# Transformer block on one core: q ahead of k in the first batch, row loads from one queue, dummy transposes around the projections, and new places for jobs of the first and last batches

## The reference, cut to what matters

```python
xn = _layernorm(x, axis=-1)
q, k, v = (split_heads(einsum('bsh,oh->bso', xn, w) * s + b) for w, s, b in ...)
scores = jnp.einsum('bhqd,bhkd->bhqk', q, k) / jnp.sqrt(jnp.float32(HEAD))
ctx = jnp.einsum('bhqk,bhkd->bhqd', jax.nn.softmax(scores, axis=-1), v)
attn = einsum('bsh,oh->bso', ctx, w_o) * s_o + b_o
h = jnp.concatenate([xn, -xn], axis=-1)
h = jax.nn.relu(s0 * (h @ w0)) * 2
h = jax.nn.relu(s1 * (h @ w1)) * 2
x = x + attn + s2 * (h @ w2)
```

## Time and profile before

| | us |
|---|---|
| median of three timed runs (296.8 to 298.94) | 297.9 |
| profiled execution, its own time | 294.85 |
| span of the profiled execution | 293.0 |
| PE busy | 273.5 (93%) |
| DVE busy | 246.0 (84%) |
| ACT busy | 219.3 (75%) |
| POOL busy | 151.0 (52%) |

### The profile page before, as it was taken

How to read it: one execution, slowest core, us unless ns; L and a number is a source line. 1 busy time by engine, 2 the same in 40 slices (tenths; PEclk the granted TensorE clock), 3 DMA queues, 4 the chain that set the end, 5 groups by cost and what they waited for, 6 DMA issues and landing times.

```text
span 293.0 us, 10539 instructions
## 1 busy us (share of the span) xinstructions
PE 273.5 (93%) x3924; PEld 185.3 (63%) x3924; DVE 246.0 (84%) x495; ACT 219.3 (75%) x456; POOL 151.0 (52%) x376
## 2 busy tenths in 40 slices
PE   4659699999999999999999999999999999999893
PEld 4235375757676776767585867677676758675442
DVE  4654969998989899998989898999999898999522
ACT  2431349889888888979888888888897988777880
POOL 6045446464929293746657382927475575421311
PEclk9557989999999999999999999999999999999999
DMA  5032403232323324142413232332424132320001
GB/s 134 28 122 60 144 19 113 62 111 68 100 76 86 112 58 131 51 126 67 127 36 112 80 106 91 97 101 57 130 60 120 42 106 74 107 74 4 22 22 36
DMA packets 27395, 23.95 MB, mean 82 GB/s; under 512 B 4674, under 2 KB 24146, under 8 KB 27346
## 3 DMA queue, kind: packets, MB, share of 16 engines
q1 hardware_dynamic: 27218, 22.89, 26.2%
q10 hardware_dynamic: 128, 0.39, 0.4%
...
## 4 chain that ended last, share of the span: by engine, by line
PE 88%; DVE 6%; ACT 2%; issue 1%; ACTq 1%; DMA 1%; POOL 0%; POOLq 0%
PE work L984 21%; PE work L1057 20%; PE max_bank L965 14%; PE exp_bank L970 9%; PE work L1089 5%; PE work L1030 4%; PE work L1014 3%; PE work L1098 3%; PE work L1021 3%; DVE neg_max L725 2%; PE work L1010 2%; PE work L999 2%; PE work L992 2%; DVE r_lo L752 1%; PE work L1009 1%
## 5 line engine op out<-in xcount | busy, mean ns | idle before, releaser
L725 DVE TENSOR_REDUCE neg_max<-max_bank 128x2 f32<-128x512 f32 x256 | 167.9, 678 | 22.0 <-PE max_bank L965 18.7
L566 ACT ACTIVATE probs<-exp_bank 128x512 f32<-128x512 f32 x256 | 145.4, 597 | 27.2 <-PE exp_bank L970 22.6
L965 PE MATMUL max_bank<-k_rows,q_rows 48*128 48x256 f16 x512 | 88.7, 271 | 1.5 <-DVE neg_max L725 1.3
L970 PE MATMUL exp_bank<-q_rows,k_rows 51*128 51x256 bf16 x512 | 87.6, 271 | 1.3 <-ACT probs L566 1.2
L984 PE MATMUL work<-probs,v_ext 128*32 128x256 f32 x1024 | 65.0, 383 | 0.2
L1057 PE MATMUL work<-r_hi,w 64*128 64x256 f16 x512 | 61.5, 274 | 0.1
L1057 PE MATMUL work<-r_lo,w 64*128 64x256 f16 x512 | 61.2, 273 | 0.0
L965 PEld LDWEIGHTS max_bank<-k_rows,q_rows 48*128 48x128 bf16 x512 | 40.2, 95 | 25.4 <-DVE neg_max L725 13.8
L970 PEld LDWEIGHTS exp_bank<-q_rows,k_rows 51*128 51x128 f16 x512 | 39.5, 94 | 9.5 <-ACT probs L566 3.3
L752 DVE SCALAR_TENSOR_TENSOR r_lo<-work,r_hi 128x512 f16<-128x512 f32 x64 | 43.3, 679 | 1.7 <-ACT r_hi L619 1.7
L619 ACT ACTIVATE r_hi<-work 128x512 f16<-128x512 f32 x64 | 36.9, 603 | 9.5 <-PE work L1057 3.9
...
## 6 DMA issues: line engine op xcount, KB each, us to landing
...
q_scratch<-q_part SPq DMA_DIRECT2D x16, 192.0 KB, 2.0
...
q_rows<-max_rows SPq DMA_DIRECT2D x64, 6.0 KB
...
```

What stands on the lines that cost most here:

```text
L566: nc.scalar.activation(probs[h // HALF][:, h % HALF, :, :].rearrange("p k q -> p (k q)"), exp_bank[h % 2][:, :], ACT.Exp, scale=EXP_SCALE) ...
L725: nc.vector.tensor_reduce(out=neg_max[:, h // HALF, h % HALF // 2, h % 2, :], in_=max_bank[h % 2][:, :].rearrange("p (q k) -> p q k", q=TT ...
L965: last = mm(max_bank[h % 2][:, t * SEQ:(t + 1) * SEQ], q[:, t * P:(t + 1) * P], k, start=True, stop=True)
L970: last = mm(exp_bank[h % 2][:, t * SEQ:(t + 1) * SEQ], k[:, t * P:(t + 1) * P], q, start=True, stop=True)
```

## The change

In batch 0, ACT scales and cuts q ahead of k; SP stores q ahead of k and also issues the four k loads, behind the q loads; DVE computes the rest of q ahead of the weights of layer 0, and both low parts ahead of the statistics of batch 1. On PE, four transposes of the identity stand between turn_x and the projections of batch 0, 22 more behind the bias matmul, and all of them write max_bank[1]. In the tables, all four quarters of layer 1 of batch 0 stand ahead of the first maxima score, with turn_x of batch 1 between the third and the second, and the projections of batch 1 behind the fourth. The low part r1_lo of the first half stands ahead of the first neg_max. maxT1 goes to bank 2 (with q and the contexts) instead of bank 0. In the batches between, some jobs change places on POOL, SP and DVE (xT_lo later on POOL; rows and max1 earlier on SP; o behind layer 2 on PE). In the last batch, maxT1 comes a head earlier, v_ext is copied later, and y on POOL stands behind the last ctxn.

```diff
@@ tables @@
-PE_LATER = {("l1_0", 0): -3, ("l1_0", 15): -1, ("l0_1", 0): -2, ("o", 14): 3, ("l0_0", 0): -2, ("xT", 0): -1, ("xT", 1): -5,
...
+            ("xT", 1): -5, ("l2", 15): -2, ("maxT1", 15): -1, ("l1_0", 0): -14, ("l1_0", 1): -1, ("l1_0", 15): -1,
...
-BANK = {"l0a": 0, "l0b": 3, "l1a": 3, "l1b": 1, "q": 2, "k": 0, "ctx0": 2, "ctx1": 2, "maxT0": 1, "maxT1": 0, "xT": 0, "v": 0,
+BANK = {"l0a": 0, "l0b": 3, "l1a": 3, "l1b": 1, "q": 2, "k": 0, "ctx0": 2, "ctx1": 2, "maxT0": 1, "maxT1": 2, "xT": 0, "v": 0,
@@ SP @@
             load_x(1)
+            store_q(sp, 0)
             store_k(sp, 0)
-            store_q(sp, 0)
             load_q(sp, 0)
+            load_k(sp, 0)
@@ ACT @@
-            scale_k(0)
-            cut_k_hi(0)
             scale_q(0)
             cut_q_hi(0)
+            scale_k(0)
             cut_q_mid(0)
+            cut_k_hi(0)
             second_layer_weights(1)
-            load_k(act, 0)
@@ DVE @@
             split_xT(nc.vector, dve, 0)
+            rest_q(nc.vector, dve, 0)
+            first_layer_weights()
+            split_q(nc.vector, dve, 0)
             split_k(nc.vector, dve, 0)
-            first_layer_weights()
-            rest_q(nc.vector, dve, 0)
             token_stats(1)
-            split_q(nc.vector, dve, 0)
             mean_and_variance(1)
@@ PE @@
-                    nc.tensor.transpose(exp_bank[0][:, 0:P], ident[:, :], ident[:, :])
+                    nc.tensor.transpose(max_bank[1][:, 0:P], ident[:, :], ident[:, :])
...
             turn_x(0)
+            keep_warm(4)
             project_qk(0, 0)
             project_qk(0, 1)
             pe.wait_ge(bv_cols_ready, 1)
             mm(exp_bank[1][:, 0:HID], bv_cols[:, :], w_sb[:, 3, :], start=True, stop=True).then_inc(bias_psum, 1)
+            keep_warm(22)
```

62 lines of the change are left out of this document (30 added, 32 removed), and 6 rows, old and new, of the table PE_LATER.

## The result

The changed kernel is slower: the median of four runs is 301.02 us (299.42 to 302.54), that of the kernel before in the same session 297.35; the ratio is 1.016, with a 95% interval of 1.0116 to 1.0204. In this document a median takes all runs of a kernel, and a ratio leaves out those more than 1.5% above the fastest run of their kernel. The profiled execution took 300.83 us, its span is 299.0. So the change costs 3.7 by the medians and 4.8 by the ratio, where the prediction had a gain of 2.0.

What follows compares the result with a forecast made beforehand. PE's own work bounds the middle, so the head was the lever: the first exp score moves from 42.20 to 40.2, a gain of 2.0, with 0 behind it, so 297.9 becomes 295.9 us; range 293.7 to 299.2.

Steps and rivals of the forecast that it cites:

- Step 8: Slots 0 to 17, first neg_max to first exp score: 15.1 us instead of 16.23, with a clock fall as today.
- Step 7: Row loads on one queue: rows land at 23.4, wait up to 0.6 covered by DVE; first neg_max at 25.1.
- T17: Start of the first exp score, slot 17; forecast at 40.2 us, against 42.20 in the kernel before.
- Behind T17: After the first exp score: 0 taken, by DVE's spare time of 14 in 190; possible loss 1.5 us together.
- Steps 1 to 3: Head: four transposes free, projections and bias at full clock to 10.23, 22 transposes 4.68 us to 14.91.
- Steps 5 and 6: Head: layer 1 starts at about 17.5, runs whole until about 21.6; batch 1's projections end at 22.85.
- The tail: Batch 15: y behind the last ctxn ends at 289.60, before the last outs at 290.17; costs 0, bound 0.7.
- B: Head rival: clock falls at 8.5, returns midway through the 22 transposes; T17 43.4, time 299.1 us, chance 0.20.
- C: Head rival: clock falls and the 22 transposes don't bring it back; T17 47.5, time 303.2 us, chance 0.08.
- D: Rival: head's gain lost to later batches (1.5), rows (0.5) or max rows; time 297.9 us, chance 0.09.

Runs made afterwards that it cites:

- e2: The kernel before with the 4 and 22 dummy transposes alone, nothing else of the change: 294.74 us, ratio 0.9953.
- e6: The changed kernel's straight code and dummies, with all ten tables and the bank of maxT1 from the kernel before: 294.96 us.
- e8: e2 with 11 dummy transposes added in the last 17 slots: 295.13 us.
- e7: e2 with the third and fourth quarters of layer 1 ahead of the first maxima score and r1_lo ahead of the first neg_max: 297.10 us, ratio 1.0008.
- e13: e6 with batch 0's layer 1, then batch 1's projections, ahead of the first maxima score, batch 1's turn_x moved, r1_lo ahead of the first neg_max: 297.41 us.
- e4: The changed kernel with 11 dummy transposes in the last 17 slots, its head unedited: 300.22 us.
- e11: The changed kernel with the old slots of batches 14 and 15 on PE, ACT and DVE: 301.44 us.
- e3: The changed kernel with 28 more dummy transposes between the maxima scores of batch 0: 302.57 us.
- e12: e6 with the changed tables of POOL and SP: 296.91 us.
- e14: The changed kernel with layer 1's last quarters, batch 1's projections and turn, its layer 0 and v among batch 0's slots, r1_lo later: 299.50 us.
- e17: e14 with the old tables of POOL and SP too: 296.99 us, ratio interval 0.9956 to 1.0043.

## Why the prediction was wrong

The direction failed, and with it the range: 301.0 lies above 299.2, and no case of the prediction had this mechanism. The step that failed is the eighth, slots 0 to 17 (15.1 predicted, 16.90 measured), with the seventh ahead of it, the first neg_max (25.1 predicted, 26.54 measured), and the term behind T17 (0 predicted, 1.75 measured). The profiled executions side by side:

| kernel | first maxima score | first neg_max | from there to T17 | half clock in it, about |
|---|---|---|---|---|
| before | 25.55 | 25.97 | 16.23 | 3.5 |
| prediction | 23.4 | 25.1 | 15.1 | 3.5 |
| changed | 24.73 | 26.54 | 16.90 | 13.5 |
| e2 | 23.53 | 23.96 | 15.64 | 3.5 |
| e6 | 23.75 | 24.17 | 16.09 | 3.5 |
| e8 | 24.66 | 25.08 | 17.40 | 7 |
| e7 | 26.96 | 28.40 | 16.05 | 10 |
| e13 | 26.68 | 29.07 | 15.82 | 10 |

- Steps 1 to 3, the dummies. Right in what they do: layer 0 starts at 15.20 (14.91 predicted), straight behind them, and ran at full clock. That the start is hit so well is luck, for two errors cancel: the projections and the bias matmul ran at the pace of half clock, and the 22 transposes started at 11.80 and not at 10.23; and they took 3.46, not 4.68. Alone the dummies gain 1.4 to 1.8 (e2), against 2.0 that the prediction gave to the whole.
- Steps 5 and 6, to the end of the projections of batch 1: 22.85 predicted, 24.36 measured. Layer 1 started at 18.53 and not at 17.5: it accumulates into the bank from which the second r_lo is read, so it waits for both r_lo. And a quarter that follows a quarter takes 1.11 from start to start, not the 0.89 that the earlier trace rows show between scores.
- Step 7, rows and first neg_max. The q store was issued at 14.32, not 12.7, because the projections were still at half clock; the k rows landed near 24.7 and not 23.4. No run shows the 1.7 that the prediction took from the issue of a load to its landing: the last k load was issued by 22.19, and PE's wait for the k rows ended at 24.73, 2.5 later. The first neg_max came at 26.54, not 25.1. What was missed is not only the size but what it does: the prediction let DVE be late and called the rows' wait covered. PE, with layer 1 done, had nothing left to do during that lateness except two scores. Against e6, which leaves this work among the scores, T17 of the changed kernel is 3.18 later, and 2.37 of that are there at the first neg_max.
- Step 8. Taking two quarters of layer 1 out of the slots was booked as a saving of PE time in a stretch that DVE sets. It took away the work with which PE had filled its waits. With it gone PE idles for over 2 us at the first neg_max, and some 13.5 us at half clock follow. The prediction expected a fall near the length of today's and bounded T17 by 41.4; measured are 43.4 to 46.8 in the changed kernel and in those with its head unedited (e4, e11). e7 and e13 show that these places, without the rest of the new tables, make the first neg_max and T17 late, with the long wait and some 10 us at half clock. What half clock costs in the slots shows in e8, which has the head of e2: 17.40 with some 7 us of it, 15.64 with 3.5. In e7 and e13 the slots take no longer than before (16.05, 15.82): that fits half clock taking back what the moved quarters had saved there, and T17 is late by about as much as the first neg_max. That the wait is what brings the fall is not shown; in e3 the clock fell with the wait cut to 0.66.
- Behind T17. Zero was taken, with 1.5 as the bound; the profiles show 1.75, and e12 has 1.46 over e6 for POOL and SP alone. The spare time of DVE was the wrong row to lean on. PE's idle time between T17 and the last maxima score grows from 0.43 to 1.52, of which 1.02 are waits for q rows, which come through POOL and SP, and the first maxima score of a batch has nothing beside it to hide that; the other 0.66 is PE's own work taking longer in its new order.
- The tail. y behind the last ctxn cost nothing, as predicted: the last output still waited for the projection (0.80 of idle, 0.81 before). The 3.0 of the profile after are no part of the change.
- The rivals. The first half of B came true: the projections ran at half clock, and the transposes started at 11.80, where B has 11.85. But the clock was back for the transposes, and layer 0 started at 15.20, not at 18.2; that B's T17, 43.4, is the measured one is luck. B and C also price a transpose at half clock at 0.425, twice the 0.2 that e2 shows (in the last section). The clock that the change lost, it lost behind layer 1. D named rows and max rows as a place of loss, at 0.5 and 1.5, but as a way to lose the gain and not more.

The sum as the runs give it, by medians over before: the dummies with the changed straight code 1.2 down (e6), the places ahead of slot 0 2.2 up (e13), POOL and SP 1.4 up (e12), which is 2.4 up of the 3.7 measured; 1.3 is left for ACT's order, PE's and DVE's later places and what the parts do to each other. By the ratios the same three are 0.4 down, 1.3 up and 0.8 up, 1.7 of 4.8, and more is left. Taken off the changed kernel, the two parts (the four places of e14, and the order on POOL and SP) give 4.0 of its 3.7 back (e17), while each alone gives 0.5 and 1.2: they are not independent. So it is shown that these two carry the loss, and their single sizes stay open within about 1 us, as does why either one alone keeps most of it.

The best version here is e2, the dummies alone in the kernel before: 0.9953 (0.9919 to 0.9987); e8 equals it.
